# Query tiles copied out of PSUM by ScalarE, the cosine product moved to GpSimd and the sine products one head later

## The reference, cut to what matters

```python
# reshaped for B, S, L = 2, 128, 128 in a helper; here B = 4 batches of S = L = 256
H, K, D_C, D_CQ, R = 16, 128, 64, 192, 64
q_hk  = (hidden_q @ Wq.T).reshape(B, S, H, K)
q_big = einsum('bshk,hkq->bshq', q_hk, w_kc_q)          # (B, S, 16, 192)
q_big = q_big * cos_q + rotate_half(q_big) * sin_q      # rotate_half: [-x[96:], x[:96]]
...
# scores against the rotated keys, softmax, context, output projection Wo
```

## Time and profile before

| | |
|---|---|
| median of 3 runs | 564.42 us (563.31 to 566.25) |
| the profiled execution, time / span | 562.89 us / 561.0 us |
| TensorE matmul / weight load busy | 457.6 us (82%) / 347.4 us (62%) |
| VectorE / ScalarE / GpSimd busy | 416.6 (74%) / 263.4 (47%) / 228.8 us (41%) |
| mean granted TensorE clock | 0.917 |
| chain that ended last, by engine | PE 45%, DVE 32%, issue 8%, ACT 5%, POOL 3% |

### The profile page before, as it was taken

One profiled execution on the slowest core, in us unless ns is written; L12 is line 12 of the kernel. 1 busy time (PEld: TensorE's weight loads), 2 busy tenths in 40 slices (PEclk: granted clock), 3 DMA queues, 4 the chain that ended last, 5 costly groups with the idle time before them and its releaser, 6 DMA issues.

```text
span 561.0 us, 11696 instructions
## 1 busy us (share of the span) xinstructions
PE 457.6 (82%) x4501; PEld 347.4 (62%) x4506; DVE 416.6 (74%) x953; ACT 263.4 (47%) x590; POOL 228.8 (41%) x236
## 2 busy tenths in 40 slices
PE   4486777576867999989897988988756999999991
PEld 2354544345745777777776877766643777777781
DVE  4079999998635888887998779786643778887860
ACT  0464336564324566655453545554412456666630
POOL 3048232322221232242255222441135288777775
PEclk9996578988878999999998999998787899999997
DMA  8990059000080000000024000100001367676613
GB/s 277 285 344 13 0 164 347 2 1 1 1 259 5 2 2 2 2 2 1 2 62 167 2 2 1 40 22 7 20 20 56 90 188 196 194 199 190 174 20 44
DMA packets 37864, 47.79 MB, mean 85 GB/s; under 512 B 7472, under 2 KB 32944, under 8 KB 37616
## 3 DMA queue, kind: packets, MB, share of 16 engines
q1 hardware_dynamic: 29728, 41.05, 22.6%
q0 software_dynamic: 4224, 4.79, 5.4%
q10 hardware_dynamic: 3856, 1.18, 0.9%
HBM read 41.18 MB, written 8.55 MB: 89 GB/s over the span
## 4 chain that ended last, share of the span: by engine, by line
PE 45%; DVE 32%; issue 8%; ACT 5%; ACTq 3%; POOL 3%; another core or an unknown queue 1%; DMA 1%; POOLq 0%; DVEq 0%
PE psum L1763 9%; PE psum L1508 6%; PE psum L1776 6%; PE psum L1599 3%; DVE lw L1025 3%; DVE lw L980 2%; PE psum L1559 2%; PE psum L1639 2%; PE psum L1566 2%; ACT lw L714 2%; DVE nmax L1067 2%; PE psum L1613 2%; DVE lw L1072 2%; DVE lw L1024 2%; DVE lw L1023 2%
## 5 line engine op out<-in xcount | busy, mean ns | idle before, releaser
L494 POOL TENSOR_TENSOR lw<-lw 128x512 f32<-128x512 f32 x48 | 60.7, 1269 | 155.7 <-DVE lw L1025 145.4
L1508 PE MATMUL psum<-lp 128*128 128x256 f16 x576 | 70.7, 278 | 4.5 <-DVE lw L1061 1.6
L714 ACT ACTIVATE lw<-psum,nmax 128x256 f32<-128x256 f32 x128 | 59.3, 469 | 27.6 <-DVE nmax L1067 27.6
L721 ACT ACTIVATE lw<-psum 128x512 f16<-128x512 f32 x64 | 38.3, 598 | 58.3 <-PE psum L1599 58.2
L1508 PEld LDWEIGHTS psum<-lp 128*128 128x128 f16 x576 | 55.2, 100 | 12.7 <-DVE lw L1061 1.8
L1763 PE MATMUL psum<-lw,se 128*128 128x320 f16 x384 | 57.4, 309 | 6.0 <-DVE lw L1284 4.8
L1072 DVE TENSOR_TENSOR lw<-psum,lw 128x512 f16<-128x512 f32 x64 | 43.6, 681 | 24.6 <-ACT lw L721 24.5
L555 POOL TENSOR_TENSOR lw<-lw 128x320 f16<-128x320 f32 x64 | 47.8, 749 | 26.8 <-DVE lw L1284 23.5
L1599 PE MATMUL psum<-identf,lw 128*128 128x128 f32 x256 | 42.3, 290 | 18.6 <-DVE lw L1072 13.2
L789 ACT ACTIVATE lw<-psum,b1w 128x320 f16<-128x320 f32 x64 | 33.7, 527 | 48.4 <-PE psum L1763 48.4
L1763 PEld LDWEIGHTS psum<-lw,se 128*128 128x128 f16 x384 | 37.6, 100 | 24.2 <-DVE lw L1284 5.5
(11 more groups left out here) (205 smaller groups left out, 987.0 us busy)
## 6 DMA issues: line engine op xcount, KB each, us to landing
se<-in_w SPq DMA_DIRECT2D x16, 1024.0 KB
dispatch<-in_empty SPq DMA_DIRECT2D x4, 662.5 KB, 10.6
lw<-dispatch SPq DMA_DIRECT2D x8, 265.0 KB
lp<-in_Wq SPq DMA_DIRECT2D x2, 1024.0 KB, 18.5
se<-in_WoT SPq DMA_DIRECT2D x1, 2048.0 KB, 13.2
lp<-in_w_kc_q SPq DMA_DIRECT2D x2, 768.0 KB, 15.7
x_sb<-in_x SPq DMA_DIRECT2D x2, 512.0 KB, 5.7
se<-in_gate_wT SPq DMA_DIRECT2D x1, 1024.0 KB, 9.2
```

Source lines behind the costliest of these rows:

```text
L494: nc.gpsimd.tensor_tensor(rope[:, c % QT, :], t1[:, c % 2, :], t2[:, c % 2, :], ALU.add)\
L714: A_(e_sb[:, n % 2, st * S:(st + 1) * S], bank[3 + n % 2][:, st * S:(st + 1) * S], ACT.Exp, bias=nmax[:, n % 2, st:st + 1], accum_out=esum ...
L1508: ins = M(tile_bank(c)[:, half * S:(half + 1) * S], m1[w][:, kc, half, col:col + P], (yth, ytl)[a][:, kc, b * S:(b + 1) * S], start=(n == ...
```

## The change

ScalarE copies each query tile from PSUM into a new SBUF buffer `qraw` of four tiles (`t1` is given up, and the space of 4 KB ahead of it). From there VectorE makes the two sine products, and GpSimd the cosine product, to which it then adds the sines in place. TensorE's waits for a free bank go to the copy. In VectorE's loop the sines of `tiles_at(n)` are made in step n + 1, behind `norm`: those of c0 at h = 3, those of c1 and c2 at h = 0 of the next group. `latent` stays where it is.

```diff
-        w2([4 * 256])
-        t1 = w2([2, 512])
+        qraw = w2([4, 512])
         t2 = w2([2, 512])
...
             def rotate(c):
-                pool.wait_ge(v_t2, 2 * c + 2)
-                pool.wait_ge(v_t1, c + 1)
+                pool.wait_ge(a_q, c + 1)
                 if c >= QT:
                     pool.wait_ge(p_qz, c // QT)
-                nc.gpsimd.tensor_tensor(rope[:, c % QT, :], t1[:, c % 2, :], t2[:, c % 2, :], ALU.add)\
+                link(nc.gpsimd.tensor_tensor(rope[:, c % QT, :], qraw[:, c % 4, :], cosq[:, c % QT, :], ALU.mult))
+                pool.wait_ge(v_t2, 2 * c + 2)
+                nc.gpsimd.tensor_tensor(rope[:, c % QT, :], rope[:, c % QT, :], t2[:, c % 2, :], ALU.add)\
                     .then_inc(g_rope, 1)
...
+            def tile_out(c):
+                act.wait_ge(p_qb, c + 1)
+                if c >= 4:
+                    act.wait_ge(g_rope, c - 3)
+                A_(qraw[:, c % 4, :], tile_bank(c)[:, :], ACT.Copy).then_inc(a_q, 1)
...
+                if s >= NT:
+                    tile_out(s - NT)
...
+            tile_out(2)
             qz_high(0)
+            tile_out(3)
             yth_of(B - 1)
+            tile_out(4)
+            tile_out(5)
             exps(0)
...
                 if h == 1 and g + 1 < NGB:
                     qz_high(g + 1)
+                for c in tiles_at(n):
+                    tile_out(c)
...
-                dve.wait_ge(p_qb, c + 1)
+                dve.wait_ge(a_q, c + 1)
                 if c >= 2:
                     dve.wait_ge(g_rope, c - 1)
-                r = tile_bank(c).rearrange("p (h s) -> p h s", h=2)
+                r = qraw[:, c % 4, :].rearrange("p (h s) -> p h s", h=2)
...
-                V.tensor_tensor(t1[:, c % 2, :], tile_bank(c)[:, :], cosq[:, c % QT, :], ALU.mult).then_inc(v_t1, 1)
...
-                for c in tiles_at(n):
+                for c in tiles_at(n - 1) if n >= 1 else ():
                     turn(c)
...
-                    pe.wait_ge(v_t1, c)
+                    pe.wait_ge(a_q, c)
                 if t == 2:
-                    pe.wait_ge(v_t1, c - 1)
+                    pe.wait_ge(a_q, c - 1)
```

More of the change, by code:

```diff
@@ L275, in program @@
         v_kr, p_kr, a_kr, v_krl = sem("v_kr"), sem("p_kr"), sem("a_kr"), sem("v_krl")
-        p_qb, v_t1, v_t2, g_rope = sem("p_qb"), sem("v_t1"), sem("v_t2"), sem("g_rope")
+        p_qb, a_q, v_t2, g_rope = sem("p_qb"), sem("a_q"), sem("v_t2"), sem("g_rope")
         p_qz, a_qz, v_qz = sem("p_qz"), sem("a_qz"), sem("v_qz")
@@ L1646, in route_turn @@
                 pe.wait_ge(v_y3, TPB * (b + 1))
-                pe.wait_ge(v_t1, min(QT * (NG * (b + 1) + 3), QT * NGB))
+                pe.wait_ge(a_q, min(QT * (NG * (b + 1) + 3), QT * NGB))
                 for it in range(TPB):
@@ L1655, in route_logits @@
                 pe.wait_ge(a_yT3, b + 1)
-                pe.wait_ge(v_t1, min(QT * (NG * (b + 1) + 4), QT * NGB))
+                pe.wait_ge(a_q, min(QT * (NG * (b + 1) + 4), QT * NGB))
                 for t in range(TPB):
@@ L1665, in route_count @@
                 pe.wait_ge(v_oh, b + 1)
-                pe.wait_ge(v_t1, min(QT * (NG * (b + 1) + 5), QT * NGB))
+                pe.wait_ge(a_q, min(QT * (NG * (b + 1) + 5), QT * NGB))
                 oh2 = ohs[:, :, :].rearrange("p a b -> p (a b)")
```

## The result

The changed kernel takes 645.2 us (median of 4, 641.0 to 651.1) against 564.1 us: ratio 1.1403, interval 1.1334 to 1.1472. The forecast was 652 us (615 to 672), slower. The ratios leave out executions that are over 1.5% above their kernel's fastest, here the profiled one (651.08 us, span 649.2; the other three average 643.8) and in run 1 too (625.13), so stretches read from these two profiles are a little longer than usual.

What follows compares the result with a forecast made beforehand. TensorE was taken to bound the attention loop. Stalls of 55.7 us, 9.5 of smaller terms and 23.1 for its clock made 88.3; 562.9 + 88.3 = 651.2, predicted as 652 us (615 to 672).

Steps and rivals of the forecast that it cites:

- The ring through `norm` and GpSimd: Attention loop, `turn_scores` of head 0 to `latent`: sines behind `norm`, then GpSimd's queue, take 7.4 us instead of 3.14.
- the shared access: Attention loop: GpSimd's add of c1 and VectorE's two-SBUF-input sines of c2 hinder each other, 0.4 us (0 to 0.8).
- the weight splits: Four groups (heads 8, 12, 16, 32): VectorE's 1.22 us split falls between GpSimd's operations, 4 x 1.2 = 4.8 us.
- the update groups: Three groups with the state update before `at_low`: one GpSimd operation more each, 3 x 1.3 = 3.9 us.
- 0.8 was for the first `latent`: First `latent`: a copy and a second GpSimd operation in front, less VectorE's shorter queue, 0.8 us.
- The clock: Attention loop: TensorE runs at 1.2 GHz for a stretch after each `latent` wait, 14 x 1.65 = 23.1 us.
- ScalarE's copy: Attention loop: the copy per tile lies beside TensorE's work and costs 0; without cover 0.6 us a tile.
- That the clock stays up: Rival: same stalls in the attention loop, TensorE stays at 2.4 GHz, about 629 us; chance 0.19.
- each wait costs 3.0 us by the clock: Rival: TensorE's clock stays low for the long stretch each time, 14 x 3.0 = 42, so 671 us; chance 0.13.
- The relief of VectorE: Rival: VectorE's 1.8 us less work a group removes 9.5 us of loop gaps, rotation hidden, about 555 us; chance 0.05.
- A plain group: Sign in the profile after: a plain four-head group of the attention loop lasts 18 to 20 us.
- the chain goes through GpSimd: Sign in the profile after: the chain of work that ended last goes through GpSimd, where it hardly did.

Runs made afterwards that it cites:

- run 1: Changed kernel with the sines made in the same step as before, copy and GpSimd cosine kept: 616.67 us, ratio 1.0913.
- Run 7: Changed kernel, sines still one step later but read from the PSUM bank behind ScalarE's copy: 659.93 us, ratio 1.1712.
- run 6: Changed kernel with the sines in the same step as before and read from the PSUM bank behind ScalarE's copy: 568.78 us, ratio 1.0094.
- run 3: Changed kernel with GpSimd's multiplies of c1 and c2 both put ahead of the two adds: 633.41 us, ratio 1.1233.
- run 4: Changed kernel with 20 filler products on TensorE ahead of the wait for `latent` in groups 2 to 15: 624.78 us, ratio 1.1084.
- run 5: Changed kernel with GpSimd's multiplies ahead of the adds and 16 filler products on TensorE ahead of `latent`: 612.46 us, ratio 1.0834.
- run 9: Changed kernel with sines in the same step as before, read from PSUM, and tile c1 made a step earlier: 560.05 us, ratio 0.9915.

## Why the prediction was right, point by point

- *The ring through `norm` and GpSimd.* Right in mechanism and size. I had 2.47 + 0.75 + 0.13 + 3.97 + 0.06 = 7.4 us and 0.4 for the shared access; the groups with nothing else in them show 7.47. Fourteen stretches were to go from 53.5 to 109.2 us, or 118 with the weight splits and the update groups; they went to 111.2. Run 7 keeps the ring and has the same stretch, runs 1 and 6 take the sines out of it and shorten it, and run 3 takes one operation out.
- *The shared access.* The mechanism was seen, its side was not. In the late place GpSimd is not stopped (0.1 us, not 0.4), VectorE's second sine is: 1.07 us, at a time when nobody waits for VectorE. The weight splits cost 0.86 us each, not 1.2. And ahead of the loop, where the sines and the multiply of a tile start together, each of the tiles 1 to 5 costs VectorE 1.07 us or more. The sum has nothing for that: its 0.8 was for the first `latent`, which came 0.5 us later behind the first query product (19.3 against 18.8), but the stretch from there to the second `latent` grew by 4.4 us. In three other runs with the same work up to there it grew by 2.5 (runs 3 and 4) and 4.4 (run 5); in runs 6, 7 and 9, without the shared access, it is 1.7 shorter than before. The Trainium skill (SBUF — State Buffer, Who interferes with whom) says that a VectorE instruction with two SBUF inputs contends with a GpSimd one that reads SBUF, and that the order of issue decides which of the two is blocked. The traces agree: 0.42 us become 1.48 when the sine starts under a multiply or an add of 1.27.
- *The update groups.* 3.9 us forecast; `turn_scores` to `latent` is 8.18 us there against 7.47, 2.1 in all.
- *The clock.* 14 x 1.65 = 23.1 us forecast. The stretches behind `latent` grew by 21.9, and run 4, with the clock at 1.00, brings them back to 151.9 us, as long as before.
- *ScalarE's copy* at 0: right. Each takes 0.60 us, and in runs 6 and 9 it costs nothing that shows.
- *The rivals.* That the clock stays up is refuted by the window behind `latent`; that each wait costs 3.0 us by the clock, by the 21.9 us measured where that would have been 42. The relief of VectorE, the rival of the other sign, can be at most the 5 us of run 9, where two things hold: the rotation is in time for `latent`, which I had named as its condition, and the access is not shared, which I had not. Nor does it come from the gaps that the rival named: the fourteen stretches sum to 51.3 us there against 53.5.
- *The signs.* A plain group was to last 18 to 20 us: the groups last 20.2 to 20.7 us, and 20.8 to 21.6 with a weight split. That the chain goes through GpSimd can't be read from the changed kernel's page, whose chain is followed back only to 477 us, behind the loop; in run 4, where it can be followed, it goes through the add, multiply and add on GpSimd in each group.

That the sum, 88.3 us, meets the 88.2 between the two spans so closely is partly luck: 64.4 forecast against 57.6 in the fourteen stretches, 23.1 against 21.9 for the clock, 0.8 against 7.0 up to the second `latent` (2.1 of it ahead of the first tile), nothing against 1.7 at the end. Against the three other executions, 79 us above the kernel before, the forecast is 9 us too long.

## What to carry to other kernels

When a step is moved later on an in-order queue, lay out everything that stands between its new place and the first reader, on every engine, and compare that with the reader's margin: here 1.1 us of margin met a chain 4.3 us longer, and the work saved didn't matter. Where work is split between VectorE and GpSimd, look at where their operands lie and at who starts first; one operand left in PSUM was worth 46 us here in the early place. In the late place the same edit made the kernel 17 us slower, since the late sines then hold a bank that TensorE wants. And a wait of TensorE cost twice here: the time, and the slower clock behind it.

## What the runs showed of the hardware

- VectorE and GpSimd stop each other in both directions: the second sine 0.42 to 1.48 us under GpSimd's multiply or add; a weight split 1.22 to 2.28; GpSimd's add 1.27 to 2.12 behind a split. With one of VectorE's two inputs in PSUM (run 6), the 48 second sines take 410 to 418 ns and the multiplies 1260 to 1280.
- Idle time of 4 to 5 us on TensorE was followed by 1.2 GHz every time, at 21.9 us over the fourteen groups; useless products in the idle time kept 2.4 GHz over the whole loop and made the kernel 3% faster.
